# Softmax probabilities divided by their sums on VectorE, one instruction for each query half, in place of GpSimd, in the attention stages of a four-layer decoder

## The chip, the cores and the metric

The kernel is one program on one core of a Trainium2 chip. It computes a whole decoder of four layers in one launch. The metric is the device time of one execution in microseconds (us); lower is better. A run's time is compared as a median over several executions.

## What is computed

The reference adds twelve blocks to a residual stream x of 8 rows (batch entries) of 256 tokens and 256 features: in each layer a self-attention or state-space block, a cross-attention block and a feed-forward block. Three of the twelve are multi-head softmax attentions that share one helper in the kernel, and only these are touched here. Cut to what matters:

```python
x = x + _L1_attn_ref(_layernorm(x), ...)                 # stage L1a: 16 heads of 16, causal
x = x + _L1_xattn_ref(ctx_1024, ctx_1024, _layernorm(x), mask, ...)   # stage L1x: 16 heads of 16
...
x = x + _L3_xattn_ref(ctx_1024, _layernorm(x), mask, ...)             # stage L3x: 8 heads of 64, 512 keys
...
# in each of the three:
score = jnp.einsum('nqhd,nkhd->nhqk', q, k)              # scaled and masked
attn = jax.nn.softmax(score, axis=-1)                    # exp(s - max) / sum
out = jnp.einsum('nhqk,nkhd->nqhd', attn, v) @ Wo
```

The division by the sum of each query's exponentials is the operation that the change moves.

## The kernel before

The program is a sequence of stages, each a block with one instruction stream per engine, kept in step by semaphores that are written by hand. At the end of a stage all engines meet, so the stages' times add up. The three attention stages are one function, `softmax_attention`, called with different sizes.

Inside a stage the work is a list of 128 items, 16 for each of the 8 rows. In L1a and L1x an item is one head with both halves of its queries (tokens 0 to 127 and 128 to 255, the two "segments"); its probabilities fill a tile `p` of 128 partitions and 384 columns (L1a: 128 keys for the first half, 256 for the second) or 512 columns (L1x: twice 256). In L3x an item is one head with one query half, 512 keys, one segment. Items run in steps of G = 4 (L1a and L1x, 32 steps) or G = 2 (L3x, 64 steps).

An item g passes through the engines like this:

- TensorE multiplies queries and keys into a PSUM bank (`scores`, L949).
- VectorE scales and masks it into `s` (`scale_mask`, L1162 or L1165) and takes the negated maximum (`maximum`, L1175 or L1177).
- ScalarE writes `p` = exp(s - max) and the sum `rsum` (`exponent`, L1059).
- VectorE inverts the sum (`reciprocal`, L1184), RLAG = 4 items behind its own `scale_mask` (3 in L3x).
- GpSimd multiplies `p` by the inverse in place (L1103 where the segments are equally long, L1107 where not) and raises the semaphore `divided`.
- TensorE waits for a free bank and for `divided`, and transposes `p` in blocks of 128 columns into that bank (`transposes`, L960).
- The bank is copied to `pT`: by ScalarE (`take_turned`, L1068), but in L1a and L1x the last item of each step by VectorE (`take_turned`, L1153).
- TensorE multiplies `pT` and the values (`weigh`, L982).

There are only two banks for transposes, queries and values together; each new use waits until the use before the last was copied out.

The order on each engine is fixed by its own loop. TensorE, in step u of L1a and L1x: transposes of the first two items of step u-1; the output projection of the row before, once a row (L934); `weigh` of step u-2; one unit of projections for the next row (keys L916, queries L902 or values L923); `scores` of step u+1; transposes of the last two items of step u-1. VectorE's loop goes item by item:

```python
for g in range(total + 2 * G):
    ...
    if RLAG <= g < total + RLAG:
        reciprocal(g - RLAG)
    if g + 1 < total and d < G - 1:
        scale_mask(g + 1)
    if g < total:
        maximum(g)
    if g + 1 < total and d == G - 1:
        ...                      # key projection of the next row, L1144 or L1141
        scale_mask(g + 1)
    if twins == 2 and d == 1 and g > G + 2:
        take_turned(g - G - 2)
```

So VectorE copies the last item of step u-2 out of its bank (L1153) in the second iteration of step u, and TensorE's transposes of the second item of step u-1 need exactly that bank.

Of the kernel before, what the change touches and what calls it, by code (L numbers as in the profile page):

```python
# [18 lines left out]
P = 128  # L19
# [14 lines left out]
ALU = mybir.AluOpType  # L34
AX = mybir.AxisListType
ROWS = 8
# [677 lines left out]
def softmax_attention(c, tag, H, rows, MQ, KT, DV, kind, scale, norm=None):  # L714
# [13 lines left out]
    nc, w = c.nc, c.dram  # L728
    NK, C = KT * P, H * DV
# [7 lines left out]
    if twins == 2:  # L737
        segs = [(0, 0, P), (1, P, 2 * P)] if causal else [(0, 0, NK), (1, NK, NK)]
        items = [(2 * (G * m + g) + e, segs) for m in range(H // 2 // G) for e in range(2) for g in range(G)]
    else:  # L740
        items = [(G * m + g, [(t, 0, NK)]) for m in range(H // G) for t in range(TB) for g in range(G)]
    n, S = len(items), len(items[0][1])
    W = sum(nk for _, _, nk in items[0][1])
    PER_ROW = n // G
    LA, NP, NPT, NSB, RLAG = (1, 8, 8, 6, 4) if twins == 2 else (2, 6, 4, 4, 3)
    total, steps = ROWS * n, ROWS * n // G
# [14 lines left out]
    with ExitStack() as stack:  # L761
# [7 lines left out]
        p_sb = [sb(f"p{i}", [P, W]) for i in range(NP)]  # L769
        pT = [sb(f"pT{i}", [P, W]) for i in range(NPT)]  # L770
        nmax = [sb(f"nmax{i}", [P, n, S]) for i in range(2)]
        rsum = [sb(f"rsum{i}", [P, n, S]) for i in range(2)]
# [32 lines left out]
        if kind == "decay":  # L805

            sig = Signals(nc, tag + "_rh")
            with nc.Block() as block:
                @block.vector
                def _(dve):  # L810
                    ch = Chain(dve, sig("dve_chain"))
                    for h in range(H):
                        nc.vector.tensor_scalar(rhat[:, h, P:], dist[:, P:], wh[:, h:h + 1], -1.0, ALU.mult, ALU.mult).then_inc(sig("minus_wr"), 1)
                    dve.wait_ge(sig("exped"), 1)
                    nc.vector.tensor_scalar(ev[:], ev[:], 1.0, scale, ALU.add, ALU.mult).then_inc(sig("numerator"), 1)
                    for h in range(H):
                        dve.wait_ge(sig("exped"), h + 2)
                        ch.link(nc.vector.tensor_scalar(rhat[:, h, P:], rhat[:, h, P:], 1.0, None, ALU.add))
                        nc.vector.reciprocal(rhat[:, h, P:], rhat[:, h, P:]).then_inc(sig("inverse"), 1)
# [23 lines left out]
        if twins == 2:  # L843
            sig = Signals(nc, tag + "_z")
# [8 lines left out]
        sig = Signals(nc, tag)  # L853
        with nc.Fori(0, B // ROWS) as turn:
            with nc.Block() as block:
# [236 lines left out]
                    output(ROWS - 1)  # L1092
                    root(ROWS - 1)

                @block.gpsimd
                def _(pool):
                    for r in range(ROWS):
                        for i, (h, segs) in enumerate(items):
                            g = r * n + i
                            pool.wait_ge(sig("reciprocal"), g + 1)  # L1100
                            if len({nk for _, _, nk in segs}) == 1:
                                both = p_sb[g % NP][:].rearrange("p (e s) -> p e s", e=S)
                                last = nc.gpsimd.tensor_tensor(both, both, rsum[r % 2][:, i, :].unsqueeze(2).to_broadcast([P, S, NK]), ALU.mult)  # L1103
                            else:
                                for e, (t, at, nk) in enumerate(segs):
                                    one = p_sb[g % NP][:, at:at + nk]
                                    last = nc.gpsimd.tensor_tensor(one, one, rsum[r % 2][:, i, e:e + 1].to_broadcast([P, nk]), ALU.mult)  # L1107
                            last.then_inc(sig("divided"), 1)

                @block.vector  # L1110
                def _(dve):
                    ch = Chain(dve, sig("dve_chain"))
                    vec = nc.vector

                    def slice_c(r):
                        src = c.ctxn if kind == "latent" else c.ctxT
                        vec.tensor_copy(cb[r % 2][:], src[:, :, bass.ts(row_of(r), T)]).then_inc(sig("sliced_c"), 1)

                    def hide(r):

                        if kind == "decay":
                            return
                        dve.wait_ge(sig(f"mask{r % 2}"), 16 * (r // 2 + 1))
                        b_, m_ = bias[r % 2], mask[r % 2]
                        if kind == "pairs":
                            ch.link(vec.tensor_scalar(b_[:], m_[:], 0.0, -1.0, ALU.not_equal, ALU.add))
                            vec.tensor_scalar(b_[:], b_[:], 1e20 * scale, None, ALU.mult).then_inc(sig("bias"), 1)
                            dve.wait_ge(sig("bias"), r + 1)
                        if kind == "latent":
                            vec.memset(b_[:, :, T:NK], 0.0)  # L1130
                            ch.link(vec.tensor_scalar(b_[:, :, 0:T], m_[:], 0.0, -1.0, ALU.not_equal, ALU.add))
                            vec.tensor_scalar(b_[:, :, 0:T], b_[:, :, 0:T], 3e38, None, ALU.mult).then_inc(sig("bias"), 1)
                            dve.wait_ge(sig("bias"), r + 1)
# [35 lines left out]
                    def maximum(g):  # L1169
                        r, i = divmod(g, n)  # L1170
                        dve.wait_ge(s_ring.emptied, g + 1)
                        s, nm = s_sb[g % NSB], nmax[r % 2]
                        if causal:
                            for e, (t, at, nk) in enumerate(items[i][1]):
                                last = vec.tensor_reduce(nm[:, i, e:e + 1], s[:, at:at + nk], AX.X, ALU.max, negate=True)  # L1175
                        else:
                            last = vec.tensor_reduce(nm[:, i, :], s[:].rearrange("p (e s) -> p e s", e=S), AX.X, ALU.max, negate=True)  # L1177
                        last.then_inc(sig("max"), 1)

                    def reciprocal(g):  # L1180
                        r, i = divmod(g, n)
                        dve.wait_ge(sig("exp"), S * (g + 1))
                        rs = rsum[r % 2][:, i, :]
                        vec.reciprocal(rs, rs).then_inc(sig("reciprocal"), 1)  # L1184

                    proj = out_bank[:].rearrange("p (t d) -> p t d", t=TB)
                    rowwise = lambda a: a[:].unsqueeze(1).to_broadcast([P, TB, D])

                    def spread(r):

                        dve.wait_ge(sig("projected"), r + 1)
                        if r:
                            dve.wait_ge(sig("added"), r)
                        for t in range(TB):
                            last = vec.bn_stats(stats[:, t, :], proj[:, t, :])
                        ch.link(last)
                        for t in range(TB):
                            last = vec.bn_aggr(mv[:, t, :], stats[:, t, :])
                        ch.link(last)
                        vec.tensor_scalar_add(rstd[:, :, 0], mv[:, :, 1], 1e-5).then_inc(sig("var_eps"), 1)  # L1200
# [28 lines left out]
                    for g in range(total + 2 * G):  # L1229
                        r, i = divmod(g, n)  # L1230
                        u, d = divmod(g, G)
                        if i == 2 and r + 2 < ROWS:
                            slice_c(r + 2)
                        if i == 3 and r + 1 < ROWS:
                            hide(r + 1)
                        if i == (LA + 2) * G and 0 < r < ROWS and kind == "latent":
                            spread(r - 1)
                        if i == (LA + 2 + (kind == "latent")) * G and 0 < r < ROWS:
                            output(r - 1)
# [3 lines that stand above are left out]
                            scale_mask(g + 1)  # L1243
                        if g < total:
                            maximum(g)
                        if g + 1 < total and d == G - 1:
                            for r_, what, i_ in units_at(u):
                                if what == "k":
                                    project(r_, i_)
# [3 lines that stand above are left out]
# [7 lines left out]
def layer1_attn(c):  # L1260
    softmax_attention(c, "L1a", 16, 16, 2, 2, 16, "decay", 0.25)


def layer1_xattn(c):
    softmax_attention(c, "L1x", 16, 16, 2, 2, 16, "pairs", 0.25)
# [1768 lines left out]
```

## Time and profile before

| | before |
|---|---|
| median of 3 runs | 4227.33 us (4219.07 to 4234.78) |
| the profiled execution, its own time | 4189.84 us |
| its span, first to last instruction | 4188.1 us |
| TensorE busy | 3185.3 us, 76% of the span |
| VectorE busy | 2399.8 us, 57% |
| ScalarE busy | 1724.2 us, 41% |
| GpSimd busy | 742.4 us, 18% |
| mean granted TensorE clock | 0.874 of full speed |

The profile is one execution. Its names for the engines are PE (TensorE matmul), PEld (TensorE weight load), DVE (VectorE), ACT (ScalarE), POOL (GpSimd) and SP (the queue of transfers). Busy shares are averages over all stages. A granted clock of 1.00 is 2.4 GHz, 0.50 is 1.2 GHz. A row of a timeline has the start in us, the duration in us, engine, line, operation, written tile, read tiles and a count; brackets at its end give the idle time of the engine just before it, and what ended that.

### The profile page before, as it was taken

What the parts mean: (1) busy time and instruction counts of PE and PEld (TensorE: products, weight loads), DVE (VectorE), ACT (ScalarE), POOL (GpSimd) and SP (SyncE); (2) the same over time, 40 slices, a digit from 0 to 9 for tenths busy, and PEclk for the clock granted to TensorE, in tenths of its full rate; (3) what the DMA queues carried; (4) which work ended last, traced back from release to release, by engine and by line L of the source; (5) the groups of instructions that cost most, each with busy time, mean ns of one, the idle gap of its engine ahead of it and who ended that gap; (6) DMA issues with size and microseconds to landing.
All of it is one profiled execution on the core that took longest, in us unless ns stands there. A gap on an engine that the chain in (4) does not pass through costs nothing. (4 is left out here: it accounts for less than half of the span.)

```text
span 4188.1 us, 55801 instructions
## 1 busy us (share of the span) xinstructions
PE 3185.3 (76%) x19029; PEld 2264.5 (54%) x19029; DVE 2399.8 (57%) x5086; ACT 1724.2 (41%) x4136; POOL 742.4 (18%) x855
## 2 busy tenths in 40 slices
PE   5999999999958787377677572487496537999797
PEld 4667676766646576244444430434396325555475
DVE  5665666566446523666666669798412675555523
ACT  4666566655432222366566521121232114555321
POOL 0000000000110232344344300000110002333332
PEclk8999999999988799689888885798798769999899
DMA  3111100110010366000000000000385000000276
GB/s 103 36 31 33 41 26 31 33 41 26 11 36 1 120 239 232 14 1 1 22 9 4 23 0 0 3 0 7 144 298 203 0 0 25 2 1 1 101 233 226
DMA packets 96627, 247.18 MB, mean 59 GB/s; under 512 B 15936, under 2 KB 62272, under 8 KB 91360
## 3 DMA queue, kind: packets, MB, share of 16 engines
q1 hardware_dynamic: 87520, 219.82, 15.5%
q0 software_dynamic: 8688, 23.78, 1.5%
q8 instruction: 154, 2.52, 0.3%
q14 instruction: 121, 0.99, 0.1%
q10 hardware_dynamic: 144, 0.07, 0.0%
HBM read 204.47 MB, written 39.15 MB: 58 GB/s over the span
## 5 line engine op out<-in xcount | busy, mean ns | idle before, releaser
L2678 POOL TENSOR_TENSOR L0a_sum_sq<-L0a_sum_sq,L0a_sq 128x512 f32<-128x512 f32 x56 | 87.1, 1555 | 1073.2 <-ACT L0a_sq L2623 1073.2
L2714 DVE SCALAR_TENSOR_TENSOR L0a_xf<-L0a_xc,L0a_conv,L0a_xf 128x256 f32<-128x256 f32 x432 | 198.5, 528 | 119.8 <-ACT L0a_xf L2588 118.6
L1103 POOL TENSOR_TENSOR L3x_p<-L3x_p,L3x_rsum 128x512 f32<-128x512 f32 x128 | 133.2, 1041 | 560.6 <-DVE L3x_rsum L1184 560.6
L2723 DVE TENSOR_TENSOR L0a_ru<-bank,L0a_um 128x512 f32<-128x512 f32 x128 | 88.1, 688 | 240.0 <-PE bank L2486 220.5
L2499 PE MATMUL bank<-L0a_ru,L0a_vm 128*128 128x256 f32 x512 | 184.2, 442 | 0.0
L1165 DVE SCALAR_TENSOR_TENSOR L3x_s<-bank,L3x_bias 128x512 f32<-128x512 f32 x128 | 86.6, 681 | 156.7 <-PE bank L949 156.7
L1103 POOL TENSOR_TENSOR L1x_p<-L1x_p,L1x_rsum 128x512 f32<-128x512 f32 x128 | 133.2, 1041 | 193.4 <-DVE L1x_rsum L1184 193.4
L1756 PE MATMUL bank<-L2a_half,L2a_diag 128*128 128x512 f32 x328 | 144.2, 601 | 28.0 <-ACT L2a_diag L1739 28.0
L2414 PE MATMUL bank<-x_feat,L0a_wx 128*128 128x256 f32 x576 | 147.6, 405 | 14.5 <-DMA L0a_wx<-in_L0a_wx 13.4
L2553 ACT ACTIVATE L0a_ex<-bank,L0a_nb 128x256 f32<-128x256 f32 x256 | 120.9, 472 | 80.0 <-PE bank L2500 78.4
L1107 POOL TENSOR_TENSOR L1a_p<-L1a_p,L1a_rsum 128x128 f32<-128x128 f32 (+1 forms) x256 | 124.3, 507 | 152.1 <-DVE L1a_rsum L1184 147.6
L230 ACT ACT_TABLE_LOAD x7 | 9.0, 1283 | 338.7 <-PEq L56 338.7
L960 PE MATMUL bank<-ident,L1x_p 128*128 128x128 f32 x512 | 88.1, 312 | 79.2 <-POOL L1x_p L1103 45.8
L2732 DVE TENSOR_TENSOR L0a_ex<-L0a_ex,L0a_qk 128x768 f32<-128x768 f32 x128 | 126.6, 989 | 32.3 <-ACT L0a_ex L2554 15.0
L2575 ACT ACTIVATE L0a_xc<-bank,L0a_bx 128x256 f32<-128x256 f32 x144 | 60.5, 471 | 199.7 <-PE bank L2414 199.7
L1165 DVE SCALAR_TENSOR_TENSOR L1x_s<-bank,L1x_bias 128x512 f32<-128x512 f32 x128 | 86.0, 675 | 97.2 <-PE bank L949 97.2
L2414 PEld LDWEIGHTS bank<-x_feat,L0a_wx 128*128 128x128 f32 x576 | 113.0, 202 | 40.6 <-DMA L0a_wx<-in_L0a_wx 13.6
L2497 PE MATMUL bank<-L0a_R,L0a_pick 32*128 32x128 f32 x512 | 126.5, 327 | 8.0 <-ACT L0a_ex L2554 8.0
L1059 ACT ACTIVATE L1x_p<-L1x_s,L1x_nmax 128x256 f32<-128x256 f32 x256 | 127.0, 500 | 12.5 <-DVE L1x_nmax L1177 12.1
L2497 PEld LDWEIGHTS bank<-L0a_R,L0a_pick 32*128 32x128 f32 x512 | 76.9, 187 | 82.8 <-issue 79.9
L2453 PE MATMUL bank<-x_feat,L0a_wz 128*128 128x256 f32 x512 | 121.6, 392 | 0.0
L960 PE MATMUL bank<-ident,L1a_p 128*128 128x128 f32 x384 | 66.9, 300 | 71.7 <-POOL L1a_p L1107 46.8
(715 smaller groups left out, 8508.4 us busy)
## 6 DMA issues: line engine op xcount, KB each, us to landing
L2f_wt<-in_L2f_w SPq DMA_DIRECT2D x23, 2180.0 KB, 10.4
L0f_wt<-in_L0f_w SPq DMA_DIRECT2D x39, 898.0 KB, 6.5
L3f_wt<-in_L3f_w SPq DMA_DIRECT2D x39, 768.0 KB, 5.9
L0a_wx<-in_L0a_wx SPq DMA_DIRECT2D x72, 256.0 KB, 3.1
L0a_wz<-in_L0a_wz SPq DMA_DIRECT2D x32, 512.0 KB, 4.2
L0f_xs<-rows_by_expert SPq DMA_DIRECT2D x39, 128.5 KB, 3.6
L3f_xs<-rows_by_expert SPq DMA_DIRECT2D x39, 128.5 KB, 3.2
rows_by_expert<-L0f_zeros SPq DMA_DIRECT2D x4, 1028.0 KB, 11.0
```

Of the source, the lines that this page charges most:

```text
L960: last = nc.tensor.transpose(bank[:, to * P:(to + 1) * P], p_sb[j % NP][:, b * P:(b + 1) * P], c.ident[:])
L1059: nc.scalar.activation(p_sb[g % NP][:, at:at + nk], s_sb[g % NSB][:, at:at + nk], ACT.Exp, bias=nmax[r % 2][:, i, e:e + 1], accum_out=rsum ...
L1103: last = nc.gpsimd.tensor_tensor(both, both, rsum[r % 2][:, i, :].unsqueeze(2).to_broadcast([P, S, NK]), ALU.mult)
L1107: last = nc.gpsimd.tensor_tensor(one, one, rsum[r % 2][:, i, e:e + 1].to_broadcast([P, nk]), ALU.mult)
L1165: ins = vec.scalar_tensor_tensor(out=s[:], in0=bank[:, 0:W], scalar=scale, in1=bias[r % 2][:].rearrange("p t s -> p (t s)"), op0=ALU.mult, ...
L1756: last = nc.tensor.matmul((odd_banks(k) if i == 1 else both_banks(k))[q][:], diag[:, k, n, :], moved(i, k, j)[:, q * 4:(q + 1) * 4, :], st ...
L2414: last = mm(bank[:, j * T:(j + 1) * T], wx[q % 3][:, k, j * P:(j + 1) * P], x(k), start=(k == 0), stop=(k == KD - 1))
L2453: last = mm(bank[:, d * T:(d + 1) * T], wz[b % 2][:, k, i * P:(i + 1) * P], x(k), start=(k == 0), stop=(k == KD - 1))
L2497: mm(bank[:, P:2 * P], pick8[rows, j, :], R8[r % 2][rows, h // 8, :], start=True, stop=True)
L2499: mm(within, vm[:], ru[g % 2][:, j, :].rearrange("p (b t) -> p b t", b=2), start=True, stop=False)
L2714: vec.scalar_tensor_tensor(out=xf[q % 4][:, j, :], in0=xc[q % 3][:, j, i:i + T], scalar=conv[:, 2 * p + j, i:i + 1], in1=xf[q % 4][:, j, : ...
L2732: vec.tensor_tensor(ex[g % 2][:], ex[g % 2][:], qk[g // NPH % 2][:].unsqueeze(1).to_broadcast([P, 2, 3 * P]), ALU.mult).then_inc(sig("att" ...
```

## The change

The whole GpSimd block of the helper goes. VectorE gets a new step, `divide`, which it runs after `maximum` for the item that `reciprocal` just dealt with. GpSimd's form was one tensor-by-tensor multiplication over the whole of `p` in L1x and L3x and one for each segment in L1a; VectorE's form is one tensor-by-scalar multiplication for each segment: 128 and 256 columns in L1a, twice 256 in L1x, 512 in L3x.

```diff
-                @block.gpsimd
-                def _(pool):
-                    for r in range(ROWS):
-                        for i, (h, segs) in enumerate(items):
-                            g = r * n + i
-                            pool.wait_ge(sig("reciprocal"), g + 1)
-                            if len({nk for _, _, nk in segs}) == 1:
-                                both = p_sb[g % NP][:].rearrange("p (e s) -> p e s", e=S)
-                                last = nc.gpsimd.tensor_tensor(both, both, rsum[r % 2][:, i, :].unsqueeze(2).to_broadcast([P, S, NK]), ALU.mult)
-                            else:
-                                for e, (t, at, nk) in enumerate(segs):
-                                    one = p_sb[g % NP][:, at:at + nk]
-                                    last = nc.gpsimd.tensor_tensor(one, one, rsum[r % 2][:, i, e:e + 1].to_broadcast([P, nk]), ALU.mult)
-                            last.then_inc(sig("divided"), 1)
...
                         vec.reciprocal(rs, rs).then_inc(sig("reciprocal"), 1)
+
+                    def divide(g):
+                        r, i = divmod(g, n)
+                        dve.wait_ge(sig("reciprocal"), g + 1)
+                        for e, (t, at, nk) in enumerate(items[i][1]):
+                            one = p_sb[g % NP][:, at:at + nk]
+                            last = vec.tensor_scalar(one, one, rsum[r % 2][:, i, e:e + 1], None, ALU.mult)
+                        last.then_inc(sig("divided"), 1)
...
                         if g < total:
                             maximum(g)
+                        if RLAG <= g < total + RLAG:
+                            divide(g - RLAG)
                         if g + 1 < total and d == G - 1:
```

The stream of VectorE shows the move. This is one step of L1x on VectorE before, from the first `scale_mask` of the step (tile `s2`) to the copy of a transposed item (`pT7`) and the reciprocal behind it; the number behind a tile's name is its buffer.

```order
L1165 SCALAR_TENSOR_TENSOR L1x_s2<-bank0,L1x_bias1 128x512
L1184 RECIPROCAL L1x_rsum1<-L1x_rsum1 128x2
L1165 SCALAR_TENSOR_TENSOR L1x_s3<-bank1,L1x_bias1 128x512
L1177 TENSOR_REDUCE L1x_nmax1<-L1x_s2 128x2
L1184 RECIPROCAL L1x_rsum1<-L1x_rsum1 128x2
L1165 SCALAR_TENSOR_TENSOR L1x_s4<-bank2,L1x_bias1 128x512
L1177 TENSOR_REDUCE L1x_nmax1<-L1x_s3 128x2
L1153 COPY L1x_pT7<-bank5 128x512
L1184 RECIPROCAL L1x_rsum1<-L1x_rsum1 128x2
```

The same stretch of the same step with the change (line numbers are 15 lower for the old helpers; L1176 is `divide`):

```order
L1150 SCALAR_TENSOR_TENSOR L1x_s2<-bank0,L1x_bias1 128x512
L1169 RECIPROCAL L1x_rsum1<-L1x_rsum1 128x2
L1150 SCALAR_TENSOR_TENSOR L1x_s3<-bank1,L1x_bias1 128x512
L1162 TENSOR_REDUCE L1x_nmax1<-L1x_s2 128x2
L1176 TENSOR_SCALAR L1x_p0<-L1x_p0,L1x_rsum1 128x256 x2
L1169 RECIPROCAL L1x_rsum1<-L1x_rsum1 128x2
L1150 SCALAR_TENSOR_TENSOR L1x_s4<-bank2,L1x_bias1 128x512
L1162 TENSOR_REDUCE L1x_nmax1<-L1x_s3 128x2
L1176 TENSOR_SCALAR L1x_p1<-L1x_p1,L1x_rsum1 128x256 x2
L1138 COPY L1x_pT7<-bank5 128x512
L1169 RECIPROCAL L1x_rsum1<-L1x_rsum1 128x2
```

Two divisions, four instructions, now stand ahead of the copy, and two more divisions follow in the rest of the step. TensorE's stream is the same before and after. This is the piece that meets the VectorE step above: the last scores of one step, the transposes of the step before it, and the first multiplications with `pT`.

```order
L949 MATMUL bank3<-L1x_kT1,L1x_qT1 128x256
L960 MATMUL bank4<-ident,L1x_p6 128x128 x4
L960 MATMUL bank5<-ident,L1x_p7 128x128 x4
L960 MATMUL bank4<-ident,L1x_p0 128x128 x4
L960 MATMUL bank5<-ident,L1x_p1 128x128 x4
L982 MATMUL bank6<-L1x_pT4,L1x_v0 32x256
```

Nothing moved here. `p7` goes into bank5, VectorE's copy `pT7<-bank5` empties it, and `p1` goes into bank5 again.

## Rows read from the trace of the kernel before

**Rows 1.** L1a, L1x, L3x: length, PE PEld DVE ACT POOL busy, PEclk, DMA, GB/s.

```profile
1753.00:2025.00 272.00, 197.85 (x1644) 127.42 (x1643) 172.72 (x580) 173.14 (x661) 124.31 (x256) 0.89 0.00 1
2058.00:2380.00 322.00, 240.01 (x1770) 155.09 (x1768) 209.17 (x466) 198.69 (x659) 133.16 (x128) 0.84 0.02 5
3493.00:3910.00 417.00, 371.91 (x2366) 238.27 (x2365) 221.85 (x516) 223.03 (x473) 133.18 (x128) 0.98 0.01 1
```

**Rows 2.** Waits in L1a's window: who waited for whom, us, times, longest us.

```profile
DVE L1a_s L1162 <- PE bank L949: 82.3, 25, 5.1
PE bank L960 <- POOL L1a_p L1107: 46.8, 33, 3.1
...
PE bank L960 <- DVE L1a_pT L1153: 24.9, 31, 0.8
```

**Rows 3.** Waits in L1x's window.

```profile
DVE L1x_s L1165 <- PE bank L949: 97.2, 25, 5.4
...
PE bank L960 <- POOL L1x_p L1103: 45.8, 32, 4.2
...
PE bank L960 <- DVE L1x_pT L1153: 33.4, 30, 1.2
```

**Rows 4.** Waits in L3x's window.

```profile
DVE L3x_s L1165 <- PE bank L949: 156.7, 60, 9.7
...
PE bank L982 <- ACT L3x_pT L1068: 25.6, 57, 0.8
```

**Rows 5.** Timeline of one step of L1x, all engines, cut to the chain.

```profile
2216.76 0.69 DVE L1165 SCALAR_TENSOR_TENSOR L1x_s<-bank,L1x_bias 128x512 f32<-128x512 f32 x1 [4.19 <-PE bank L949]
2217.37 0.16 DVE L1184 RECIPROCAL L1x_rsum<-L1x_rsum 128x2 f32<-128x2 f32 x1
...
2217.60 1.04 POOL L1103 TENSOR_TENSOR L1x_p<-L1x_p,L1x_rsum 128x512 f32<-128x512 f32 x1 [4.49 <-DVE L1x_rsum L1184]
...
2218.62 0.15 DVE L1184 RECIPROCAL L1x_rsum<-L1x_rsum 128x2 f32<-128x2 f32 x1
...
2218.79 0.63 PE L960 MATMUL bank<-ident,L1x_p 128*128 128x128 f32 x4 [1.02 <-POOL L1x_p L1103]
2218.86 1.04 POOL L1103 TENSOR_TENSOR L1x_p<-L1x_p,L1x_rsum 128x512 f32<-128x512 f32 x1 [0.21 <-DVE L1x_rsum L1184]
...
2219.87 0.68 DVE L1153 COPY L1x_pT<-bank 128x512 f32<-128x512 f32 x1
...
2220.61 0.66 PE L960 MATMUL bank<-ident,L1x_p 128*128 128x128 f32 x4 [1.19 <-DVE L1x_pT L1153]
```

**Rows 6.** Timeline: the key copies of one step, in L1a and in L1x.

```profile
1926.50 1.41 DVE L1144 TENSOR_SCALAR L1a_kT<-bank,L1a_twin 128x512 f32<-128x512 f32 x2 [1.39 <-PE bank L916]
...
2224.23 1.41 DVE L1144 TENSOR_SCALAR L1x_kT<-bank,L1x_twin 128x512 f32<-128x512 f32 x2 [0.51 <-PE bank L916]
```

**Rows 7.** Timeline: 16 VectorE multiplications by a per-partition scalar, back to back.

```profile
30.50 4.29 DVE L2357 TENSOR_SCALAR L0a_wout<-L0a_wout,L0a_norm 128x256 f32<-128x256 f32 x16
```

**Rows 8.** VectorE tensor-by-scalar groups by shape: busy us, mean ns of one.

```profile
L1450 DVE TENSOR_SCALAR L1f_gate<-L1f_gate,L1f_s_out 128x1536 f32<-128x1536 f32 x8 | 8.1, 1015 | 0.5
...
L1450 DVE TENSOR_SCALAR L1f_gate<-L1f_gate,L1f_s_mix 128x2048 f32<-128x2048 f32 x6 | 7.7, 1286 | 0.2
...
L212 DVE TENSOR_SCALAR n0a_xs<-x_res,n0a_mv,n0a_rstd 128x256 f32<-128x256 f32 x16 | 5.4, 408 | 1.1 <-PE bank L224 1.1
```

**Rows 9.** Durations of VectorE forms, ns min/median/max, and first and last start.

```profile
L2357 DVE TENSOR_SCALAR L0a_wout<-L0a_wout,L0a_norm x16: 348/348/349, 30.5 to 34.4; 128x256 f32<-128x256 f32 x16
...
L1117 DVE COPY L1x_cb<-ctx_feat x8: 415/418/428, 2048.4 to 2261.5; 128x512 f32<-128x512 f32 x8
...
L556 DVE TENSOR_SCALAR L0f_xn<-x_res,L0f_mv,L0f_rstd x16: 398/404/1129, 1405.0 to 1412.0; 128x256 f32<-128x256 f32 x16
```

**Rows 10.** Busy time in single microseconds of L1a, around one wait.

```profile
1913.00:1914.00 1.00, 0.06 (x1) 0.09 (x2) 1.00 (x5) 0.41 (x2) 0.93 (x3) 1.00 0.00 0
...
1916.00:1917.00 1.00, 1.00 (x13) 0.43 (x16) 0.85 (x4) 0.54 (x2) 0.93 (x3) 0.50 0.08 16
```

## The prediction

> **What bounds the three stages now.** The change touches only L1a, L1x and L3x, so I read their windows first [rows 1]. In none is GpSimd near full: 124.31 of 272 us, 133.16 of 322, 133.18 of 417. TensorE is busy 73% and 75% in L1a and L1x and 89% in L3x; VectorE 64%, 65% and 53%. No engine is full in L1a and L1x, so something else holds them: a loop of waits. The lists of waits show it. VectorE waits for TensorE's scores for 82.3 us in L1a and 97.2 in L1x [rows 2, 3], and TensorE waits for VectorE and GpSimd ahead of its transposes: 46.8 + 24.9 = 71.7 us in L1a, 45.8 + 33.4 = 79.2 us in L1x [rows 2, 3]. Each waits for the other once a step; the step is as long as the sum of both legs.
>
> One step shows the order of the leg [rows 5]. Scores arrive, VectorE starts at 2216.76. Its first reciprocal is at 2217.37; GpSimd starts 0.23 us later (2217.60), takes 1.04 us, and TensorE starts the transposes of the first item at 2218.79 after 1.02 us of waiting. The second item's product is GpSimd's from 2218.86 to 2219.90. TensorE does not start it then but at 2220.61, when VectorE's copy L1153 (2219.87, 0.68 us) has emptied the bank. So the leg ends with **VectorE's copy**, not with GpSimd, which was done 0.7 us before. This ending is there in 31 of L1a's 32 steps and 30 of L1x's [rows 2, 3].
>
> L3x is different. TensorE's largest wait there is 25.6 us for ScalarE [rows 4]; none of note is for GpSimd, and VectorE waits 156.7 us for scores, 60 times, 2.6 us each [rows 4]. TensorE's own work is the bound.
>
> **What the change removes.** All GpSimd work of the helper (133.16 us in L1x alone [rows 1]) and its hand-over of 0.2 us. As a gain on the path this is nothing: the work it hands to TensorE is ready before the bank is. The product of the first item, for which TensorE waits on GpSimd today, does not come sooner either: VectorE has it only after a `scale_mask` and a `maximum`, some 1.2 us behind the reciprocal (the pace from 2217.37 to 2218.62 in [rows 5]), and then the division itself, against 0.23 + 1.04 us now.
>
> **What it adds.** 256 instructions in L1a and L1x each, 128 in L3x, all on VectorE. The nearest row is a multiplication of 128x256 by a per-partition scalar in place: 16 take 4.29 us [rows 7], the last of them 0.348 us [rows 9], so one starts every (4.29 - 0.348) / 15 = 0.263 us. The column price is (1286 - 1015) / 512 = 0.53 ns [rows 8]. So a 128-column one takes 0.263 - 0.068 = 0.195 us, a 512-column one 0.263 + 0.136 = 0.40 us. An item costs 0.46 us in L1a, 0.53 in L1x, 0.40 in L3x. From below: VectorE's plain copy of 512 columns lasts 0.418 us [rows 9], 0.33 from start to start if the next one overlaps it by as much as in L2357 (0.348 - 0.263); less 0.13 for 256 columns, that makes 0.34 and 0.40 us an item in L1a and L1x. From above: the two-scalar form L212 at 408 ns [rows 8], start to start the same, which makes 0.75 and 0.82 us. I take L2357, the same operation with the same operands.
>
> The skill page "VectorE: DVE Perf Modes" (section "The perf-mode tier table") says that an fp32 multiplication by a scalar from SBUF runs at two elements a cycle and a tensor-by-tensor one at one. The trace agrees: 0.53 ns a column is half of the 1.04 ns of a cycle of 0.96 GHz, that page's clock. By the same page's cycle table for SBUF to SBUF (58 cycles and half a cycle a column) an item would cost an estimated 0.32 us in L1a and 0.39 in L1x, and 31 steps of two divisions 44 us, where the rows give 61.
>
> **Where it lands.** Two divisions stand ahead of the copy L1153 in VectorE's stream, as the order shows. Nothing covers them: VectorE runs without a gap from 2216.76 to the copy [rows 5], and TensorE waits at the end. L1a: 31 x 2 x 0.46 = 28.5 us. L1x: 31 x 2 x 0.53 = 32.9 us. The other two divisions of a step come behind the copy, where VectorE idles for scores (82.3 / 25 = 3.3 us and 97.2 / 25 = 3.9 us [rows 2, 3]), and cost nothing, except in the step that also projects keys. There VectorE waits only 0.51 us (L1x) or 1.39 us (L1a) for TensorE's keys and then goes on without another wait [rows 6]. VectorE comes four divisions later, TensorE two; in L1x 2 x 0.53 - 0.51 = 0.55 us stick out, seven times, 3.9 us; in L1a 0.92 is below 1.39, nothing. Behind the divisions on VectorE queue the next `scale_mask` and `maximum`, so ScalarE's exponentials come up to 0.9 us later; ScalarE is busy 64% and 62% [rows 1]. In L3x the divisions add 0.80 us to a step that has 2.6 us of waiting: nothing. The delay of the order alone is 28.5 + 32.9 + 3.9 = 65 us.
>
> **The clock.** TensorE's granted clock falls after it has waited: from 1913 to 1914 it was busy 0.06 us, and from 1916 to 1917 the clock was 0.50, 1.2 GHz, with TensorE busy throughout [rows 10]. A microsecond at half clock, all busy, costs 0.5 us. From the mean clock [rows 1] the time at half clock is (1 - 0.89) x 2 x 272 = 60 us in L1a (1.9 a step) and 0.32 x 322 = 103 us in L1x (3.2 a step), against 0.04 x 417 = 17 us in L3x where TensorE hardly waits. The waits a step are 71.7 / 31 = 2.3 us and 79.2 / 31 = 2.6 us; after the change 3.2 and 3.6 us. From below I keep the ratio of L1a (0.83 us at half clock for each us of wait): 2.7 a step in L1a, no growth in L1x, (2.7 - 1.9) x 32 / 2 = 13 us. From above the ratio of L1x (1.25): 4.0 and 4.5 a step, ((4.0 - 1.9) + (4.5 - 3.2)) x 32 / 2 = 54 us. I take 42, nearer the upper end, since both stages will wait longer than L1x does now.
>
> The Trainium skill, "TensorE: Matmul & The Clock Gate" (its Part 1), says that a hardware monitor halves the array's clock after an idle stretch. The rows named here agree with it; the price above is from them.
>
> **Sum.** 65 + 42 = 107 us. Against the profiled execution's own 4189.84 us that is 4297; that execution is 37 us below the median of the runs, so on the median 4227.33 + 107 = 4334 us, 2.5% slower.
>
> **Rivals.**
> - *The order costs, the clock does not.* The half-clock stretches grow no more than at the lower ratio, or fall into the waits: 65 to 78 us, 4292 to 4305. For it: in L1x nearly every step has such a stretch already. Against it: L1a goes past what L1x waits now. Chance 0.18.
> - *L3x is drawn in.* If the delay of ScalarE's exponentials reaches TensorE there, 64 steps x 0.8 us = 51 us more, 4385. For it: its 57 waits for ScalarE's copies [rows 4]. Against it: 2.6 us of slack a step, and ScalarE busy 53%. Chance 0.05.
> - *It is hidden.* VectorE's idle time of 82.3 and 97.2 us [rows 2, 3] would hold 128 x 0.46 = 59 and 128 x 0.53 = 68 us, and busy shares alone say no change: 4227. Against it: that idle time lies behind the copy, not ahead of it. It decides if TensorE's wait for the copy was put down wrongly. Chance 0.04.
> - *Faster: GpSimd stops holding VectorE.* A GpSimd multiplication of 1.04 us that keeps VectorE's fast forms from starting would cost up to that each time. Two such instructions a row in L1a, four in L1x and six in L3x (slices, masks, additions) make 12 x 8 = 96; if half of them met it, 50 us would come back, 4177, if the divisions hid. It can happen: L556 took 1129 ns once and 404 as a rule, with GpSimd active in between [rows 9]. Against it: in L1x all eight slices took 415 to 428 ns [rows 9], so there is nothing to come back. Chance 0.02.
>
> The skill page "SBUF — State Buffer" (section "Who interferes with whom") states such a rule: VectorE in a two-port mode and GpSimd exclude each other for a whole instruction. The maximum of L556 agrees with that Trainium skill rule; the eight slices show that this loop does not run into it.
>
> **Chances and range.** Forecast 0.71, the four rivals 0.18, 0.05, 0.04, 0.02. A difference of 0.5%, 21 us, is about what a measurement of this kernel can tell from no change. Slower by more than that: forecast, first and second rival, 0.94; I keep 0.91 for a mistake in all of them. Within: 0.05. Faster: 0.04. The lower end has the division at its lower bound, 31 x 2 x (0.34 + 0.40) = 46 us, and 13 us of clock: 4286; I write 4285. The upper bounds, 31 x 2 x (0.75 + 0.82) = 97, about 8 for the key steps and 54 of clock, give 159 us, 4386; with 1 in 10 left out above, I stop at 4370.
>
> **What would show it.** GpSimd has no instruction in the three stages. VectorE's busy time rises by about 60 to 75 us in L1a and L1x and 50 in L3x. TensorE's wait for VectorE's copy grows from 0.8 and 1.1 to about 2 us or is shared with a wait for the division, with an unchanged count of 31. L1a grows by about 50 us, L1x by about 57, L3x by less than 5, all other stages by nothing. The mean clock falls to about 0.80 in L1a and 0.79 in L1x. The prediction is wrong if a division of 256 columns takes much more or less than 0.26 us from start to start, if L3x grows, or if the clock stays where it is.

## The result and the profile after

The changed kernel took 4332.57 us (median of 4 runs, 4326.77 to 4339.88), the kernel before 4228.4 us over the 4 runs taken beside it. The ratio is 1.0249, with a 95% interval of 1.0224 to 1.0274: 104 us slower. The profiled execution took 4331.82 us.

The three stages in the trace after, in windows with the same margins as those of [rows 1] (length, busy time of PE, PEld, DVE, ACT, POOL, granted clock, DMA share, GB/s):

```profile
1773.00:2096.00 323.00, 223.50 (x1643) 142.23 (x1642) 231.46 (x835) 178.18 (x661) 0.00 (x0) 0.79 0.00 1
2129.00:2502.00 373.00, 258.39 (x1766) 164.36 (x1760) 276.51 (x721) 201.87 (x658) 0.00 (x0) 0.79 0.01 4
3614.00:4034.00 420.00, 373.90 (x2366) 239.23 (x2365) 271.95 (x644) 223.05 (x473) 0.00 (x0) 0.98 0.01 1
```

L1a went from 272 to 323 us, L1x from 322 to 373, L3x from 417 to 420. VectorE gained 59, 67 and 50 us of busy time. The clock fell from 0.89 to 0.79 in L1a and from 0.84 to 0.79 in L1x. Below, a stage is measured more sharply, from the start of its first transpose to the start of its last; the numbers are the first and last start of L960 in each trace:

| us | L1a | L1x | L3x |
|---|---|---|---|
| before | 258.6 | 305.9 | 401.7 |
| after | 309.2 | 357.0 | 404.6 |
| difference | 50.6 | 51.1 | 2.9 |

The sum is 104.6 us, as much as the medians differ. The two profiled executions differ by 142 us. The other 37 lie in code that the change does not touch: L1a's first transpose starts 20.3 us later (1782.5 against 1762.2), and 18.1 us come behind L3x (301.9 against 283.8 from the last transpose to the end of the span). They are a difference between two executions, not part of the change: e4 below has the same code up to L1a, and its first exponential there comes 18.5 us sooner than in this trace (1757.7 against 1776.2).

One step of L1x after, cut as [rows 5] (start, duration, engine, line, operation, idle time before and what ended it):

```profile
2263.04 0.69 DVE L1150 SCALAR_TENSOR_TENSOR L1x_s<-bank,L1x_bias 128x512 f32<-128x512 f32 x1 [2.77 <-PE bank L949]
2263.65 0.15 DVE L1169 RECIPROCAL L1x_rsum<-L1x_rsum 128x2 f32<-128x2 f32 x1
...
2264.90 0.61 DVE L1176 TENSOR_SCALAR L1x_p<-L1x_p,L1x_rsum 128x256 f32<-128x256 f32 x2
...
2265.42 0.16 DVE L1169 RECIPROCAL L1x_rsum<-L1x_rsum 128x2 f32<-128x2 f32 x1
...
2265.65 0.63 PE L960 MATMUL bank<-ident,L1x_p 128*128 128x128 f32 x4 [1.60 <-DVE L1x_p L1176]
...
2266.68 0.60 DVE L1176 TENSOR_SCALAR L1x_p<-L1x_p,L1x_rsum 128x256 f32<-128x256 f32 x2
...
2267.20 0.68 DVE L1138 COPY L1x_pT<-bank 128x512 f32<-128x512 f32 x1
...
2267.94 0.88 PE L960 MATMUL bank<-ident,L1x_p 128*128 128x128 f32 x4 [1.66 <-DVE L1x_pT L1138]
```

Each division holds VectorE for 0.52 us (2264.90 to 2265.42, 2266.68 to 2267.20). From the first `scale_mask` to TensorE's second transposes it is 4.90 us, against 3.85 in [rows 5]: 1.05 us more, two divisions. The waits in L1x's window after, to be held against [rows 3]:

```profile
DVE L1x_s L1150 <- PE bank L949: 83.6, 24, 4.6
...
PE bank L960 <- DVE L1x_p L1176: 63.8, 31, 4.8
...
PE bank L960 <- DVE L1x_pT L1138: 47.1, 31, 1.7
```

TensorE's two waits went from 45.8 + 33.4 to 63.8 + 47.1 us, in as many steps. Each time the first wait is 2.1 us on average and the second 1.5. VectorE still waits for scores in the other half of the step.

### The profile page after: what moved, and what is told of

Its sections match the earlier page's. It is cut to its first block and busy times, and to the rows that moved or that the text cites. A ratio compares the mean times of both kernels' runs of the same rounds, so it can differ in the third digit from the quotient of the medians.

```text
span 4330.0 us, 55929 instructions
## 1 busy us (share of the span) xinstructions
PE 3246.0 (75%) x19029; PEld 2292.5 (53%) x19029; DVE 2575.5 (59%) x5726; ACT 1732.2 (40%) x4136; POOL 351.8 (8%) x343
## 5 line engine op out<-in xcount | busy, mean ns | idle before, releaser
L960 PE MATMUL bank<-ident,L1x_p 128*128 128x128 f32 x512 | 89.0, 314 | 111.6 <-DVE L1x_p L1176 63.8
L960 PE MATMUL bank<-ident,L1a_p 128*128 128x128 f32 x384 | 72.8, 320 | 97.1 <-DVE L1a_p L1176 57.1
L960 PEld LDWEIGHTS bank<-ident,L1x_p 128*128 128x128 f32 x512 | 61.7, 155 | 138.4 <-issue 78.9
L1751 PEld LDWEIGHTS bank<-L2a_half,L2a_diag 128*128 128x128 f32 x328 | 62.5, 191 | 108.4 <-issue 77.0
L2457 PE MATMUL bank<-L0a_wout,L0a_yzT 128*128 128x256 f32 x512 | 119.0, 385 | 0.6 <-DVE L0a_yzT L2737 0.6
```

The source lines that it names most:

```text
L960: last = nc.tensor.transpose(bank[:, to * P:(to + 1) * P], p_sb[j % NP][:, b * P:(b + 1) * P], c.ident[:])
L1751: last = nc.tensor.matmul((odd_banks(k) if i == 1 else both_banks(k))[q][:], diag[:, k, n, :], moved(i, k, j)[:, q * 4:(q + 1) * 4, :], st ...
L2457: last = mm(bank[:, t * D:(t + 1) * D], yzT[:, g % NY, t * P:(t + 1) * P], wout[:, g % NPH, :], start=(d == 0), stop=(d == GRP - 1))
```

## The experiments

All times are medians; a ratio is to the kernel before, on the same chip in the same rounds, with its 95% interval. Chips differ: the kernel before took 4187.8 us beside e1 to e4, 4224.9 beside e5, e6, e7 and e9, 4194.5 beside e8, e10 and e11, and 4193.4 beside e12. The stage columns come from each run's trace, as in the table above. In e3, e4, e5, e7 and e11 a stage's first transpose comes sooner behind its first exponential (some 3 us in L1a, 4 to 5 in L1x), and their columns read that much too long beside the others. From the first exponential to the last transpose L1a and L1x take 264.4 and 313.3 us before, 315.5 and 365.0 in the changed kernel, 266.0 and 311.9 in e3, 323.1 and 369.1 in e4.

| kernel | ratio (interval) | L1a | L1x | clock in L1a, L1x |
|---|---|---|---|---|
| before | 1 | 258.6 | 305.9 | 0.88, 0.84 |
| changed | 1.0249 (1.0224 to 1.0274) | 309.2 | 357.0 | 0.79, 0.79 |
| e1_extra_each | 1.0266 (1.0247 to 1.0286) | 307.4 | 360.1 | 0.81, 0.79 |
| e2_extra_late | 1.0073 (1.0057 to 1.0090) | 273.8 | 321.9 | 0.83, 0.83 |
| e3_no_division | 1.0005 (0.9994 to 1.0015) | 263.3 | 308.7 | 0.87, 0.86 |
| e4_lag2 | 1.0276 (1.0259 to 1.0293) | 320.2 | 365.7 | 0.79, 0.79 |
| e5_early_lag2 | 0.9926 (0.9903 to 0.9949) | 241.2 | 287.8 | 0.90, 0.87 |
| e6_early_pool | 1.0084 (1.0058 to 1.0110) | 279.7 | 306.6 | 0.82, 0.84 |
| e7_early_pool_lag2 | 0.9752 (0.9735 to 0.9770) | 213.8 | 250.0 | 0.95, 0.94 |
| e8_only_l3x | 1.0003 (0.9993 to 1.0013) | 258.5 | 305.9 | 0.88, 0.84 |
| e9_filler | 1.0308 (1.0287 to 1.0329) | 327.8 | 354.5 | 1.00, 1.00 |
| e10_filler_small | 1.0043 (1.0027 to 1.0060) | 267.3 | 312.4 | 0.97, 0.96 |
| e11_earlier_lag2 | 0.9729 (0.9706 to 0.9752) | 213.2 | 244.6 | 0.95, 0.97 |
| e12_filler_before | 0.9877 (0.9853 to 0.9900) | 238.1 | 277.8 | 0.97, 0.96 |

### The place or the amount of VectorE's work: e1 and e2

The theory was that the loss is what VectorE does ahead of its copy. Its rival: the loss is the division's result being late, or VectorE's total work. Both kernels are the one before, GpSimd dividing, with multiplications on VectorE whose result nobody reads.

```diff
+                    def idle_work(g):
+                        for e, (t, at, nk) in enumerate(items[g % n][1]):
...
+                            vec.tensor_scalar(junk[:, k % 8, 0:nk], wo[:, 0, 0:nk], twin[:, 0:1], None, ALU.mult).then_inc(sig("junk"), 1)
...
                         if g < total:
                             maximum(g)
+                        # e1: each item, where the change divides
+                        if twins == 2 and RLAG <= g < total + RLAG:
+                            idle_work(g)
+                        # e2 instead: all four behind the last maximum of a step
+                        if twins == 2 and RLAG <= g < total + RLAG and d == G - 1:
+                            for _ in range(G):
+                                idle_work(g)
```

> The kernel before, GpSimd still divides; VectorE gets in L1a and L1x, at the places where the change puts its divisions, multiplications of the same shapes whose result nobody uses. If the change costs by what VectorE does ahead of its copy L1153 and not by who divides, this is as slow as the changed kernel in L1a and L1x: +105 us, ratio 1.025. If the loss came from the division's result being late, GpSimd's is as early as before and this is at the kernel before plus at most 10 us. If VectorE's two-port form and GpSimd exclude each other for a whole instruction, the extra ones are stretched by up to 1.04 us each and it is slower than the changed kernel, +150 us or more.

> The same extra multiplications as in e1_extra_each, as many, but all of a step behind its last maximum, where VectorE goes on to wait for scores (3.3 and 3.9 us a step). If the place is what counts: nothing, except in the seven key steps of each stage, where 2.1 - 0.5 = 1.6 us in L1x and 1.8 - 1.4 = 0.4 us in L1a stick out, 14 us in all: ratio 1.003. If VectorE's amount of work counts: +105 us as in e1_extra_each.

e1 gives 1.0266: the loss is that of the change, though GpSimd still divides. TensorE's waits in L1x's window of e1:

```profile
PE bank L961 <- DVE L1x_pT L1154: 68.4, 31, 2.2
...
PE bank L961 <- POOL L1x_p L1104: 46.6, 32, 4.2
```

TensorE waits for GpSimd as long as in the kernel before (46.6 against 45.8 us) and for VectorE's copy twice as long (68.4 against 33.4) [rows 3]. So it is not the division that is late, it is VectorE's stream that is longer. e2 has the same instructions, and most of the loss is gone (1.0073). It is the place that counts, though not alone: e2 loses 15.2 us in L1a and 16.0 in L1x where 3 and 11 were expected. Part of that is a stretch that the third expectation of e1 named. VectorE's extra instructions by shape, in e1 (busy us, mean ns of one):

```profile
L1193 DVE TENSOR_SCALAR L1x_junk<-L1x_wo,L1x_twin 128x256 f32<-128x256 f32 x256 | 93.6, 406 | 0.0
```

and one pair in the timelines of VectorE and GpSimd of the same execution:

```profile
2241.26 1.03 DVE L1193 TENSOR_SCALAR L1x_junk<-L1x_wo,L1x_twin 128x256 f32<-128x256 f32 x2
```

```profile
2240.84 1.04 POOL L1104 TENSOR_TENSOR L1x_p<-L1x_p,L1x_rsum 128x512 f32<-128x512 f32 x1 [0.74 <-DVE L1x_rsum L1185]
```

A pair takes 0.60 us alone and 1.03 us where GpSimd's multiplication is running as it starts; the mean of one is 406 ns, against 345 for the real divisions after. So GpSimd's form holds this one up. The Trainium skill, "SBUF — State Buffer" (section "Who interferes with whom"), says so, and this trace agrees. The stretch falls mostly behind the copy: in L1x the extra instructions ahead of it last 356 ns on average, those behind it 454. It costs e1 little. In e2 eight instructions took 2.61 us in place of the 2.1 that I had used, which explains some 0.5 us in each of the 14 key steps. The rest of e2's loss is open. Its trace has L1a's clock at 0.83 in place of 0.88 and TensorE busy 12.5 us longer there; in L1x TensorE waits for GpSimd 59.2 us in place of 45.8.

### Whether GpSimd's division cost anything: e3

```diff
-                @block.gpsimd
-                def _(pool):
...
-                        pe.wait_ge(sig("divided"), j + 1)
+                        pe.wait_ge(sig("reciprocal" if twins == 1 else "exp"), j + 1 if twins == 1 else S * (j + 1))
```

> The kernel before without any division: GpSimd's multiplications are left out, nobody takes their place, and TensorE transposes the exponentials as they are (the attention's output stays undivided). If VectorE's copy ends the leg, TensorE waits for it as before and GpSimd's 71.7 and 79.2 us of waits hide nothing but the first part of that wait: within 15 us of the kernel before, ratio 0.997 to 1.00. If GpSimd's products held TensorE: up to 93 us faster, ratio 0.978.

No gain at all: 1.0005. The waits in L1x's window of this kernel say where GpSimd's share went:

```profile
PE bank L960 <- DVE L1x_pT L1138: 67.2, 30, 3.2
```

TensorE's wait for VectorE's copy grew from 33.4 to 67.2 us and took most of the 45.8 us that it had waited for GpSimd [rows 3]. So even a division that takes no time would bring nothing in this order.

### The copy or the division as the wait after: e4

```diff
-    LA, NP, NPT, NSB, RLAG = (1, 8, 8, 6, 4) if twins == 2 else (2, 6, 4, 4, 3)
+    LA, NP, NPT, NSB, RLAG = (1, 8, 8, 6, 2) if twins == 2 else (2, 6, 4, 4, 3)
```

> The changed kernel with reciprocal and division two items behind scale_mask in L1a and L1x (RLAG 2 in place of 4). TensorE's products are then ready a step's idle time earlier, but two divisions still stand ahead of the copy L1138. If the copy is what the step waits for: as slow as the changed kernel, ratio 1.02 to 1.025. If TensorE's wait for the division (57.1 and 63.8 us) is what costs: most of the loss comes back, ratio below 1.01.

The products are ready long before TensorE needs them; the time does not come back (1.0276). It even reads a little above the change, with intervals that overlap; in the traces L1a is 7.6 us longer and L1x 4.1 from first exponential to last transpose. Why stays open. TensorE's wait in L1x's window:

```profile
PE bank L960 <- DVE L1x_pT L1138: 99.8, 31, 4.3
```

TensorE no longer waits for a division and waits for the copy for 99.8 us. The 63.8 us that the trace after gives to the division L1176 were not its price.

### What the clock costs: e9, e10 and e12

A filler keeps TensorE active in the first of its two waits. It writes into the bank that the transposes then overwrite.

```diff
                         bank = claim(("p", j))
+                        if twins == 2 and j % G == 0:
+                            for _ in range(5):          # e9: 6 of 512 columns; e12: 3, on the kernel before
+                                nc.tensor.matmul(bank[:, 0:P], c.ident[:], c.xT[:, 0, 0:P], start=True, stop=True)
                         pe.wait_ge(sig("divided"), j + 1)
```

> The changed kernel; TensorE runs six multiplications of 512 columns (0.2 us each at full clock) whose result is overwritten, in L1a and L1x once a step, in the bank of the first transposes, ahead of the wait for the division, where it waits 57.1 and 63.8 us. Nothing of the order changes. If some 42 us of the loss are half-clock time that the waits bring about: mean clock of both stages above 0.9 and 20 to 45 us below the changed kernel, ratio to the kernel before 1.014 to 1.02. If the clock costs nothing on the path: no change, 1.025; if the filler sticks out of the wait: slower.

> As e9_filler, but five multiplications of 128 columns in place of six of 512. In e9_filler one of 512 columns took 0.9 us in two instructions, so its six stuck out by over 3 us a step; five of 128 columns take about 1.1 us and fit into the 1.6 us that TensorE waits for the division at least. If the half-clock time costs: mean clock above 0.85 in both stages and 15 to 40 us below the changed kernel, ratio to the kernel before 1.016 to 1.021. If it is off the path: 1.025 with a higher clock.

> The kernel before with the filler of e10_filler_small, three multiplications in place of five, since TensorE waits only 1.02 us for GpSimd's first product and the 0.31 us of the bank's hand-over come first. It prices the half-clock time that the kernel before has itself, so that e10_filler_small less this is the order of the change alone. The prediction's terms say 65 us for the order: ratio to the kernel before 0.987 to 0.991 with e10_filler_small at 1.004. If the order cost only the 18 us that e10_filler_small shows over the kernel before, the filler gains nothing here: 1.000.

e9 was built on a wrong duration. An fp32 multiplication of 512 columns is two instructions, and the six took 5.42 us, not 1.3:

```profile
2263.25 5.42 PE L959 MATMUL bank<-x_feat,ident 128*128 128x512 f32 x12 [0.31 <-ACT L1x_pT L1071]
```

The clock was 1.00 in both stages, and L1a and L1x still took 327.8 and 354.5 us, since the filler stuck out. It shows that the filler holds the clock up, and no more.

e10's filler fits (ten instructions, 1.38 us; behind it TensorE still waits for the copy, 51.6 us in L1x), and the changed kernel falls to 1.0043. That is 86 us below the change and far more than the 15 to 40 that I had said. The reason is in e12: the kernel before has half-clock time of its own, and the filler takes that away too, 0.9877, as expected. Windows over the stages as in the table, first L1a, then L1x; e10:

```profile
1750.50:2017.80 267.30, 209.32 (x1885) 147.88 (x1886) 222.48 (x810) 172.98 (x637) 0.00 (x0) 0.97 0.01 1
2066.40:2378.80 312.40, 239.63 (x2014) 168.83 (x2014) 265.04 (x699) 197.12 (x639) 0.00 (x0) 0.96 0.02 5
```

and e12:

```profile
1766.70:2004.80 238.10, 195.01 (x1761) 134.09 (x1762) 164.23 (x556) 166.56 (x640) 123.04 (x254) 0.97 0.01 1
2052.80:2330.60 277.80, 224.79 (x1889) 154.35 (x1890) 198.96 (x447) 191.98 (x640) 131.92 (x127) 0.96 0.02 5
```

With both kernels at 0.96 to 0.97 of full clock the change costs 267.3 - 238.1 = 29.2 us in L1a and 312.4 - 277.8 = 34.6 us in L1x: 63.8 us for the order. The remaining 101.7 - 63.8 = 37.9 us are half-clock time that the longer waits bring about. The two fillers differ in length (five and three multiplications), so the split is good to a few us only. A second reading, without fillers: in the same windows of the two traces TensorE runs the same multiplications and is busy 215.64 us after against 189.96 before in L1a, 250.12 against 230.85 in L1x, 45 us more in all; that is a rougher measure of the same half-clock time.

### L3x: e8

The change in L3x alone: GpSimd's block stays for L1a and L1x.

```diff
+                if not (twins == 1):
+                    @block.gpsimd
+                    def _(pool):
...
-                        if RLAG <= g < total + RLAG:
+                        if (twins == 1) and RLAG <= g < total + RLAG:
                             divide(g - RLAG)
```

> The change in L3x alone; L1a and L1x keep GpSimd. Slack of 2.6 us a step against 0.8 us: 0 to 5 us, ratio 1.000 to 1.001. If VectorE's work counted there: 64 x 0.8 = 51 us, 1.012.

1.0003. The trace has L3x at 404.6 us against 401.7, the 2.9 us of the change itself. An additional VectorE instruction that lasts 0.48 us in every item costs 0.05 us a step where 0.8 would stand if nothing hid it.

### From the cause to a faster kernel: e5, e6, e7 and e11

If the leg to the copy sets the step, the copy should come forward, and the products must be ready by then.

```diff
-    LA, NP, NPT, NSB, RLAG = (1, 8, 8, 6, 4) if twins == 2 else (2, 6, 4, 4, 3)
+    LA, NP, NPT, NSB, RLAG = (1, 8, 8, 6, 2) if twins == 2 else (2, 6, 4, 4, 3)   # e5, e7, e11; not e6
...
                         if g < total:
                             maximum(g)
+                        if twins == 2 and d == 0 and g > G + 1:     # e11: ahead of maximum
+                            take_turned(g - G - 1)
...
-                        if twins == 2 and d == 1 and g > G + 2:
-                            take_turned(g - G - 2)
```

e5 is this on the changed kernel, e6, e7 and e11 on the kernel before, so GpSimd divides in them.

> The kernel before (GpSimd divides, RLAG 4), with only the copy moved one iteration forward. The bank is then free at 2.5 us after the first scores in place of 3.8, but the second product comes later, since its reciprocal now stands behind the copy: 2.5 + 0.2 + 1.04 = 3.75 us and the hand-over. TensorE waits for GpSimd in place of the copy: ratio 0.995 to 1.005. If the copy alone were the whole leg: 62 x 1.3 = 80 us faster, ratio 0.98.

> The kernel before with the early copy of e6_early_pool and RLAG 2, so that both products are ready before the step and only the copy is waited for, at 2.5 us in place of 3.8. Leg 1.3 us shorter in 62 steps, 80 us, and 15 to 30 us less at half clock: ratio 0.973 to 0.98. As VectorE carries no divisions it should beat e5_early_lag2 by 10 to 30 us. If ScalarE's order (its copies stand behind its exponentials) takes over as the wait: ratio 0.99 to 1.00.

> The changed kernel with RLAG 2 in L1a and L1x and VectorE's copy of the transposed item moved one iteration forward, behind the first maximum of a step. Then no division and one scale_mask, one maximum and one reciprocal less (1.3 us) stand ahead of the copy, and the products are ready before. If the leg to the copy sets the step: against the changed kernel the 1.05 and 0.92 us of divisions and the 1.3 us go, 62 x 2.3 = 140 us, and some half-clock time; but VectorE now has so much work in the key steps that some 25 us stay: 4% below the changed kernel, ratio to the kernel before 0.98. If VectorE's amount of work is the bound: ratio above 1.01.

> e7_early_pool_lag2 with the copy ahead of the first maximum of a step in place of behind it. In e7_early_pool_lag2 TensorE still waits 33.7 us for the copy in L1x; the leg becomes 0.6 us shorter: 15 to 35 us faster than it, ratio to the kernel before 0.966 to 0.972. If ScalarE, whose exponentials wait for that maximum, takes the time back: equal to it, 0.975.

e6 moves only the copy. In L1x the time stays, as expected (306.6 against 305.9): TensorE now waits for GpSimd. In L1a it loses 21.1 us, which I had not expected. The clock there fell from 0.88 to 0.82, and L1a's waits for GpSimd are now 76.8 us, 63 times:

```profile
PE bank L960 <- POOL L1a_p L1107: 76.8, 63, 3.1
```

That is 5 us more than the 71.7 of [rows 2]. The rest is slower multiplications: over the stage TensorE is busy 205.82 us in e6 and 189.96 before, 15.9 us more for the same instructions. Why waits of nearly the same sum leave the clock so much lower is open.

e7 has both moves and is 2.5% faster than the kernel before, inside its forecast; the stages fall by 44.8 and 55.9 us, and the clock rises to 0.95 and 0.94. e5, the same order with VectorE dividing, gains 0.7% only, where I had expected 2%; its rival, a ratio above 1.01, did not come either. With the order equal, VectorE costs 27.4 us in L1a and 37.8 in L1x over GpSimd, more than the 10 to 30 in all that I had said. Its waits show why, in L1x:

```profile
ACT L1x_p L1059 <- DVE L1x_nmax L1162: 51.7, 61, 2.6
PE bank L960 <- DVE L1x_pT L1138: 50.9, 30, 3.6
...
DVE L1x_s L1150 <- PE bank L949: 16.6, 15, 2.3
```

VectorE hardly waits for scores any more (16.6 us, 97.2 before) and is busy 268.88 of the 287.8 us, 93%: in this shorter step it is close to being the bound itself.

e11 brings the copy forward once more. L1x gains 5.4 us over e7, L1a 0.6, where I had expected 15 to 35. Its ratio, 0.9729, lies just outside the 0.966 to 0.972 that I had given, and its interval (0.9706 to 0.9752) reaches up to e7's value. It is the fastest kernel here, at 4077.0 us where the kernel before takes 4194.5; that it beats e7 is not certain.

## Why the prediction was right

The forecast was 4334 us; 4332.57 was measured. The mechanism held, but so close a hit is partly luck: two terms were a few us too large, L3x's 2.9 us was not in the sum, and these errors in part cancel. Point by point:

- **What bounds the stages.** That VectorE's copy ends the leg, and that GpSimd's division costs nothing in this order, is shown three ways: e3 takes the division out and gains nothing, e4 makes it early and gains nothing, e1 leaves GpSimd alone and has the whole loss.
- **The price of a division.** 0.263 us from start to start and 0.53 an item in L1x, taken from L2357; measured 0.52. The real ones last 345 ns, L2357 348. The cycle table in the Trainium skill, "VectorE: DVE Perf Modes" (section "The TRN2 errata — SBUF-src ops pay a fixed extra latency per instruction"), by which I had estimated 0.39, is too low here.
- **The order's term.** 28.5 us in L1a, 32.9 + 3.9 in L1x; measured with the clock held up 29.2 and 34.6. The 3.9 us of the key steps was not measured apart. Two slips in the working are of no weight: L1x's term counts 31 steps where [rows 3] has 30, 1.1 us, and the lower price of an item in L1a comes to 0.33, not 0.34.
- **The clock's term.** 42 us, chosen between 13 and 54; 101.7 - 63.8 = 37.9 measured. The choice in that wide range was a judgement, not a sum. Of the rise forecast for L1x, about 57 us, 51.1 came. The clocks after are 0.79 and 0.79, where 0.80 and 0.79 were forecast. The mechanism that the rows suggested, waits first and half clock then, is shown by the fillers: they change nothing but TensorE's activity in a wait, and the time falls.
- **L3x.** Nothing was forecast, 2.9 us came. TensorE waits for a division 4 times there, 2.9 us in all; that these make the stage's 2.9 us is likely and was not tested.
- **The rivals.** The order without the clock would have given 4292 to 4305; the fillers refute it. L3x drawn in: refuted by e8. Hidden by VectorE's idle time: e2 shows that most of it can be, if the work stands in that idle time, and e1 that it is not where the change puts it. GpSimd holding VectorE up: the mechanism exists (e1's stretched pairs), and e3, without any GpSimd work in the stages, shows that there was nothing to give back.

That the two profiled executions differ by 142 us and the medians by 104 is a warning: against the profiled execution's own time the sum gave 4297, and only the step to the median made it 4334.

## What to carry to other kernels

When two engines hand work to and fro once a step, an operation costs what it puts between the arrival of one engine's data and the instruction that releases the other; before moving it, find that instruction (here a copy out of PSUM, not the division that the longer wait names) and count what stands ahead of it. The same operations behind it cost under a third here, and a faster engine ahead of it can cost more than a slower one beside it. Where TensorE waits a few us in each step, price its clock too: here it was over a third of the loss, and on the kernel before 1.2% of the whole time could be had by letting TensorE multiply into a bank that is overwritten anyway.

## What the runs showed of the hardware that was not expected

- A filler of TensorE in its waits raised the granted clock: 1.38 us a step on the changed kernel, from 0.79 in both stages to 0.97 and 0.96, paid 86 us; 0.94 us a step on the kernel before, from 0.88 and 0.84 to 0.97 and 0.96, paid 52 us.
- An fp32 multiplication of 128x512 runs as two instructions and takes 0.90 us (six of them, twelve instructions, in 5.42 us); five of 128 columns are ten instructions in 1.38 us.
- A VectorE multiplication by a per-partition scalar, SBUF to SBUF, that starts while GpSimd multiplies waits for it: a pair took 1.03 us in place of 0.60, and single ones up to 1125 ns.
